# Two attention blocks on one core: the last two images rearranged over DMA queues and PSUM banks

## What is computed

```python
def stage_a(x, w_qkv, w_proj, b_proj):
    q, k, v = split(x @ w_qkv)                       # 8 heads of 32, windows of 32 tokens
    attn = softmax(q @ k.T * 32 ** -0.5)
    return (attn @ v) @ w_proj + b_proj

def stage_b(x, Wq, Wk, Wv, gamma):
    energy = einsum('bid,bjd->bij', x @ Wk, x @ Wq)  # 1024 x 1024 for each image
    return gamma * (softmax(energy) @ (x @ Wv))

x = x + stage_a(_gn(x), ...)
x = x + stage_b(_gn(x), ...)
```

## Time and profile before

| what | us |
|---|---|
| median of 3 runs | 668.62 |
| the 3 runs | 664.68, 668.62, 669.41 |
| profiled execution, its own time | 666.09 |
| its span, first to last instruction | 664.3 |
| PE busy | 592.8 (89%) |
| DVE busy | 467.3 (70%) |
| ACT busy | 348.4 (52%) |
| POOL busy | 198.7 (30%) |

### The profile page before, as it was taken

How to read it: one execution, slowest core, us unless ns; L and a number is a source line. 1 busy time by engine, 2 the same in 40 slices (tenths; PEclk the granted TensorE clock), 3 DMA queues, 4 the chain that set the end, 5 groups by cost and what they waited for, 6 DMA issues and landing times.

```text
span 664.3 us, 15166 instructions
## 1 busy us (share of the span) xinstructions
PE 592.8 (89%) x5859; PEld 428.8 (65%) x5859; DVE 467.3 (70%) x765; ACT 348.4 (52%) x486; POOL 198.7 (30%) x198
## 2 busy tenths in 40 slices
PE   2888855899999999999999999999999999876887
PEld 2465732457785777568776778577766767654656
DVE  4565477587867787788868787878868875754562
ACT  2664243485268644874278535865387414631462
POOL 7423322302351315320450335231442142002203
PEclk9999977799999999999999999999999999887989
DMA  6122422133224313223223313331322232201001
GB/s 204 32 58 69 125 64 62 44 78 97 71 67 111 95 27 97 81 60 108 59 75 87 95 44 91 99 87 44 97 72 57 53 81 65 52 1 58 33 0 64
DMA packets 40116, 47.53 MB, mean 72 GB/s; under 512 B 6848, under 2 KB 32064, under 8 KB 40064
## 3 DMA queue, kind: packets, MB, share of 16 engines
q1 hardware_dynamic: 35312, 41.57, 23.8%
q10 hardware_dynamic: 4624, 4.98, 2.3%
q0 software_dynamic: 128, 0.26, 0.1%
HBM read 10.09 MB, written 8.39 MB: 28 GB/s over the span
## 4 chain that ended last, share of the span: by engine, by line
PE 70%; DVE 14%; ACT 5%; issue 4%; DMA 3%; SPq 2%; ACTq 0%; POOL 0%; POOLq 0%; DVEq 0%
PE pb L296 10%; PE pb L298 9%; PE pb L297 9%; PE pa L296 6%; PE pa L297 6%; PE pa L298 6%; PE pa L576 5%; PE pb L630 4%; PE pb L648 4%; DVE max_neg L1110 3%; PE pa L543 3%; PE pb L462 2%; PE pa L462 2%; DVE bst L1005 2%; ACT e L896 1%
## 5 line engine op out<-in xcount | busy, mean ns | idle before, releaser
L296 PE MATMUL pb<-v_h,e_h 128*128 128x257 f16 x448 | 123.9, 277 | 0.0
L298 PE MATMUL pb<-v_h,e_l 128*128 128x257 f16 x448 | 122.8, 274 | 0.0
L297 PE MATMUL pb<-v_l,e_h 128*128 128x257 f16 x448 | 122.5, 273 | 0.0
L1110 DVE TENSOR_REDUCE max_neg<-pb 128x1 f32<-128x1024 f32 x64 | 77.8, 1218 | 57.8 <-PE pb L630 57.6
L1125 DVE TENSOR_TENSOR e_l<-e,e_h 128x1024 f16<-128x1024 f32 x64 | 77.9, 1224 | 19.8 <-ACT e L896 18.4
L905 ACT ACTIVATE qk_h<-pb,y_fac 128x256 f32<-128x256 f32 x56 | 26.5, 472 | 108.8 <-DVE y_fac L1132 108.4
L896 ACT ACTIVATE e<-pb,f_energy 128x1024 f32<-128x1024 f32 x64 | 71.3, 1113 | 17.0 <-PE pb L648 17.0
L1331 POOL TENSOR_TENSOR y<-qk_h,y 128x256 f32<-128x256 f32 x64 | 45.9, 724 | 104.6 <-ACT qk_h L905 104.5
L1312 POOL TENSOR_TENSOR xb<-xin,bias 128x2048 f32<-128x2048 f32 x8 | 36.3, 4532 | 120.2 <-DVE x L1090 119.5
L1317 POOL TENSOR_TENSOR before_turn<-before_turn,a_rinv 128x1024 f32<-128x1024 f32 x16 | 30.6, 1915 | 113.3 <-DVE a_rinv L1071 107.9
L630 PE MATMUL pb<-q_stack,k_stack 96*128 96x512 f16 x128 | 40.6, 400 | 17.7 <-DVE max_neg L1110 8.2
(11 more groups left out here) (153 smaller groups left out, 1373.8 us busy)
## 6 DMA issues: line engine op xcount, KB each, us to landing
diag<-qkT SPq DMA_DIRECT2D x64, 128.0 KB, 2.4
xin<-in_x SPq DMA_DIRECT2D x15, 512.0 KB, 4.8
diag<-turned SPq DMA_DIRECT2D x60, 128.0 KB, 2.4
turned<-before_turn SPq DMA_DIRECT2D x118, 64.0 KB, 2.0
out<-y SPq DMA_DIRECT2D x24, 256.0 KB, 2.2
out<-y ACTq DMA_DIRECT2D x8, 256.0 KB, 2.1
q_stack<-qk_hl SPq DMA_DIRECT2D x8, 128.0 KB, 2.3
k_stack<-qk_hl SPq DMA_DIRECT2D x7, 128.0 KB, 2.4
```

Source lines behind the costliest of these rows:

```text
L296: nc.tensor.matmul(out_ap, lh, rh, start=start, stop=False)
L297: nc.tensor.matmul(out_ap, lh, rl, start=False, stop=False)
L298: return nc.tensor.matmul(out_ap, ll, rh, start=False, stop=stop)
L1110: nc.vector.tensor_reduce(max_neg[:, it:it + 1], energy_banks(b, it).rearrange("p a n -> p (a n)"), X, ALU.max, negate=True).then_inc(b_ma ...
```

## The change

- Regrouping of image 7: rows 0 and 1 (eight DMAs) stay on SP's queue, rows 2 and 3 (eight) go to POOL's, ahead of `b_keep(6, 3)`, with a semaphore of their own (`a_oxp`). The stacks of image 7: two DMAs on SP's queue, two on POOL's (`b_stackp`).
- Projection of image 7 in pa 0 to 3, without the wait for the residual two steps back.
- Step 6 has its own order on PE, ACT and DVE: no pairs of image 6 before the projection and transposes of image 7 are done; then pairs for tiles 0 to 3; the queries and keys of image 7 in pb 2 and 3; and pairs of jt 0 to 6 for tiles 4 and 5, ahead of the first energy. ACT copies all four transposes ahead of exponential 5.
- Image 6's tiles 6 and 7 are in pa 2 and 3. Energies of image 7: tiles 2, 4 and 6 in pa 0 and 1, the others in pb 0 and 1, each waiting for the maximum two before it. Values 0 to 2 of image 7 are made in `first(7)`.
- Turned energies of image 7 alternate between pb 0, 1 and pb 2, 3 and wait for the exponential two before. Behind each exponential only tiles 0 to 3 are made; tiles 4 to 7 come at the end, eight pairs each, in pb 0 to 3.
- The last tile of image 7 is scaled and added by one DVE instruction (`b_finish`) instead of one on ACT and one on POOL.

The core of the diff (semaphore declarations and the arguments that carry a bank's name are left out):

```diff
         def proj_bank(b, j):
-            return pb[:, (2 + j) % 4, :] if image(b, 0) else pa[:, 2 + j % 2, :]
+            if image(b, 0):
+                return pb[:, (2 + j) % 4, :]
+            return pa[:, j, :] if last_image(b) else pa[:, 2 + j % 2, :]
         def energy_banks(b, it):
...
                 return pb[:, 2:4, :]
+            if last_image(b) and it > 1 and it % 2 == 0:
+                return pa[:, 0:2, :]
             return pb[:, 0:2, :]
...
+        def value_bank(b, j):
+            return pb[:, 2 + j % 2, :]
+        def qk_bank(b, c):
+            return pb[:, 2 + c, :] if last_image(b) else pb[:, c, :]
+        def energy_T_banks(b, jt):
+            return pb[:, 2:4, :] if last_image(b) and jt % 2 == 1 else pb[:, 0:2, :]
         def split3(out_ap, lhs, rhs, start=True, stop=True):
...
         def result_bank(b, it):
             if last_image(b):
-                return pa[:, it, :] if it < 4 else pb[:, (it - 2) % 4, :]
-            if next_to_last(b) and it < 4:
-                return pa[:, it, :]
+                return pa[:, it, :] if it < 4 else pb[:, it - 4, :]
+            if next_to_last(b) and not 4 <= it < 6:
+                return pa[:, it if it < 4 else it - 4, :]
             return pb[:, 2 + it % 2, :]
...
             def second(i, b, o, m, f):
                 more = f and not (isinstance(i, int) and i + 3 >= IMAGES)
-                if m: a_regroup(sp, i + 1, range(4))
+                if m: a_regroup(sp, a_ox, i + 1, (0, 1) if last_image(i + 1) else range(4))
                 if more and not m: load(i + 3)
...
                 if more and m: load(i + 3)
-                if m: b_stacks(sp, i + 1)
+                if m: b_stacks(sp, b_stack, i + 1, (0, 2) if last_image(i + 1) else range(4))
             sp.dma_start(xin[:, 0:TPC, :], x_v[0, 0:TPC].rearrange("t p c -> p t c")).then_inc(a_load[0], 16)
...
             def a_projection(b, b_next, js):
                 for j in js:
-                    regrouped(pe, b, (j % 2,))
+                    if last_image(b) and j % 2 == 0:
+                        pe.wait_ge(a_ox, nth(b - 1, 256, 128))
+                    elif last_image(b):
+                        pe.wait_ge(a_oxp, 128)
+                    else:
+                        regrouped(pe, b, (j % 2,))
                     if image(b, 0) and j >= 2:
                         pe.wait_ge(a_ve, nth(1, 4, j + 1))
-                    elif j >= 2:
+                    elif j >= 2 and not last_image(b):
                         pe.wait_ge(a_x1, nth(b, 4, j - 1))
...
                     pe.wait_ge(a_ve, nth(b, 4, 7 + c))
+                elif last_image(b):
+                    pe.wait_ge(n_["b"]["ve"], nth(b, 1, 1))
                 else:
                     after(pe, b_exp, nth(b, 8, 0))
-                project_T(pb[:, c, :], wqk1_h, wqk1_l, slice(0, P), c, b_nh, b_nl).then_inc(b_qk, 1)
+                project_T(qk_bank(b, c), wqk1_h, wqk1_l, slice(0, P), c, b_nh, b_nl).then_inc(b_qk, 1)
             def b_project_v(b, js):
                 for j in js:
-                    if j < 2:
+                    if last_image(b) and j < 2:
+                        pe.wait_ge(b_part, nth(b - 1, 8, 5 + j))
+                    elif j < 2:
                         after(pe, b_part, nth(b, 8, j - 1))
...
+                        last = project(value_bank(b, j)[:, t * CH:(t + 1) * CH], (b_nh[:, :, tok], b_nl[:, :, tok]), wv1_h, wv1_l, slice(0, CH))
                     last.then_inc(b_v, 1)
             def b_energy(b, it, b_next):
-                pe.wait_ge(b_stack, nth(b, 64, 64))
...
                     pe.wait_ge(b_max, it - 1)
+                elif last_image(b) and it == 2:
+                    pe.wait_ge(b_part, nth(b - 1, 8, 2))
+                elif last_image(b) and it > 2:
+                    pe.wait_ge(b_max, nth(b, 8, it - 1))
                 else:
...
                     pe.wait_ge(b_rows, nth(b, 1, 1))
+                elif last_image(b) and jt == 1:
+                    pe.wait_ge(b_vl, nth(b, 4, 4))
+                elif last_image(b):
+                    pe.wait_ge(b_exp, nth(b, 8, jt - 1))
                 else:
...
                 for c in range(CHUNKS):
-                    last = nc.tensor.matmul(pb[:, c, :], q_stack[0:98, jt * P:(jt + 1) * P],
+                    last = nc.tensor.matmul(energy_T_banks(b, jt)[:, c, :], q_stack[0:98, jt * P:(jt + 1) * P],
                                             k_stack[0:98, c * CHUNK:(c + 1) * CHUNK], start=True, stop=True)
...
                     pe.wait_ge(b_el, nth(b, 8, jts[-1] + 1))
+                    if it >= 4:
+                        pe.wait_ge(b_exp, nth(b, 8, 8))
+                elif next_to_last(b):
+                    pe.wait_ge(b_el, nth(b, 8, jts[-1] + 1))
                     if it >= 6:
-                        pe.wait_ge(b_exp, nth(b, 8, 8))
-                elif next_to_last(b) and it < 4:
-                    pe.wait_ge(b_el, nth(b, 8, jts[-1] + 1))
-                elif next_to_last(b):
-                    if it >= 6:
-                        pe.wait_ge(b_part, nth(b, 8, it - 1))
+                        pe.wait_ge(b_part, nth(b, 8, it - 3))
+                    elif it >= 4:
+                        pe.wait_ge(b_qkl, nth(b + 1, 2, 2))
                 elif jts[0] == 0:
...
                     last.then_inc(b_pv, 1)
+            def last_first(i):
+                b_energy(i, 0, False)
+                outputs_behind(i - 1, (7,))
+                b_energy(i, 1, False)
+                b_energy(i, 2, False)
+                b_output(i - 1, 6, True, range(0, 4))
+                b_energy(i, 3, False)
+                b_output(i - 1, 6, True, range(4, 8))
+                b_energy(i, 4, False)
+                b_output(i - 1, 7, True, range(0, 4))
+                b_output(i - 1, 7, True, range(4, 8))
+                b_energy(i, 5, False)
+                b_project_v(i, (0, 1))
+                b_energy(i, 6, False)
+                b_project_v(i, (2,))
+                b_energy(i, 7, False)
             def first(i, b, o, m, f):
+                if last_image(i): return last_first(i)
                 for it in range(4):
-                    if o and b and not next_to_last(i - 1): b_output(i - 1, it, b, range(0, 4))
-                    if next_to_last(i - 1): b_output(i - 1, 4 + it // 2, b, range(it % 2 * 4, it % 2 * 4 + 4))
+                    if o and b: b_output(i - 1, it, b, range(0, 4))
                     if b and it == 2: b_energy(i, 1, m)
-                    if o and b and not next_to_last(i - 1): b_output(i - 1, it, b, range(4, 8))
+                    if o and b: b_output(i - 1, it, b, range(4, 8))
                     if f and it == 1: transposes("a", i + 2, range(4))
...
                     if o and last_image(i - 1):
-                        if it >= 6: b_output(i - 1, it, b)
+                        b_output(i - 1, it, b)
                         continue
-                    if next_to_last(i - 1): b_output(i - 1, 4 + it // 2, b, range(it % 2 * 4, it % 2 * 4 + 4))
-                    elif o: b_output(i - 1, it, b, range(0, 4))
+                    if o: b_output(i - 1, it, b, range(0, 4))
                     if f and it == 5: group_mean("a", i + 2)
...
                     if b and it == 7: b_energy(i, it, m)
-                    if o and not next_to_last(i - 1): b_output(i - 1, it, b, range(4, 8))
+                    if o: b_output(i - 1, it, b, range(4, 8))
                     if b and it < 7: b_energy(i, it, m)
             def outputs_behind(b, jts, its=range(6)):
                 for jt in jts:
-                    if jt == 0:
-                        pe.wait_ge(b_vl, nth(b, 4, 4))
-                        pe.wait_ge(a_ol, nth(IMAGES, 2, 0))
+                    pe.wait_ge(b_vl, nth(b, 4, jt // 2 + 1))
                     for it in its:
                         b_output(b, it, False, (jt,))
+            def next_to_last_second(i):
+                b_project_v(i, (0,))
+                b_max_rows(i)
+                b_project_v(i, (1,))
+                b_energy_T(i, 0)
+                b_project_v(i, (2,))
+                b_energy_T(i, 1)
+                b_project_v(i, (3,))
+                b_energy_T(i, 2)
+                b_energy_T(i, 3)
+                a_projection(i + 1, False, (0, 1))
+                b_energy_T(i, 4)
+                a_projection(i + 1, False, (2,))
+                transposes("b", i + 1, (0, 1))
+                a_projection(i + 1, False, (3,))
+                b_energy_T(i, 5)
+                transposes("b", i + 1, (2, 3))
+                outputs_behind(i, (0, 1, 2), range(4))
+                group_mean("b", i + 1)
+                outputs_behind(i, (3,), (0, 1))
+                group_var("b", i + 1)
+                outputs_behind(i, (3,), (2, 3))
+                b_energy_T(i, 6)
+                outputs_behind(i, (4,), range(4))
+                for c in range(CHUNKS):
+                    b_project_qk(i + 1, False, c)
```

(81 more changed lines are left out.)

76 lines of the change are left out of this document (39 added, 37 removed).

## The result

| | before | after |
|---|---|---|
| median, 22 runs each | 664.5 us (663.04 to 669.41) | 661.92 us (659.48 to 664.58) |
| ratio after to before | | 0.9947, 95% interval 0.9933 to 0.9962 |
| span of the profiled execution | 664.3 us | 660.4 us |

The ratio is 3.5 us on 664.5; the two medians alone differ by 2.6 us. The kernel is faster by half a per cent, less than the 1% that was named as the bound between "faster" and "the same", and it is clear of zero only because 22 runs stand on each side.

What follows compares the result with a forecast made beforehand. PE bounds the kernel, busy 89% of the span, with 28.0 us idle or at half clock after 557.6 us. A span gain of 5.6 less 1.3 for half clock gives 668.62 - 4.3 = 664.3 us, range 659.3 to 669.0.

Steps and rivals of the forecast that it cites:

- Regrouping: Image 7's regrouping DMAs, on two queues, land at 567.3 and 567.7 us; PE wants them at 569.0.
- third rival: POOL's regrouping DMAs held up by DVE, 2.5 us an issue, projection 1 9.7 us late: 674.0 us; chance 0.03.
- Projection: Projection of image 7: half clock kept up to 572.7 us, last transposes end at 579.1, before 583.2.
- Normalisation: Image 7's statistics chain: `normalise` starts at 586.2 instead of 593.0, 6.8 us earlier; 2.1 us given away ahead of `group_mean`.
- PE as the bound: First energy of image 7 at 601.5 instead of 605.6, stacks there before; with fewer pairs left, 7.4 us ahead.
- Energies: Image 7's energies up to the row maxima: `b_max_rows` at 619.1 against 624.0; 7.5 us ahead so far.
- Turned energies of image 7: Last image's exponentials: circle of 5.4 us over two jt, 3.55 of it PE work; of 7.5 us ahead 4.8 left.
- Half clock: PE's clock falls once in the last image, costing 1.3 us of the 5.6 us span gain.
- The end: Last matmul to store: one DVE instruction, issue at 656.0 to 656.1; span ends at 658.7, 5.6 us less.
- (1): No cost by the clock, as the fall comes where PE waits anyway: 5.6 us gain, 663.0 us; chance 0.2.
- (2): Clock falls again and again in the last image and once at 589: 1.2 us gain, 667.4 us; chance 0.15.
- (4): More gain than summed: hand-placed waits of 1 us are shorter, up to 3 us: 661.3 us; chance 0.19.

Runs made afterwards that it cites:

- group mean early: Changed kernel with image 7's group mean behind eight pairs of image 6 instead of twelve, and the group variance behind twelve: median 662.54 us, ratio 0.9973.
- filled gaps: Changed kernel with matmuls that feed nothing put into two of PE's gaps in the last image (14 and 20): median 660.52 us, ratio 0.9954.

## Why the prediction was right, point by point

The forecast was 4.3 us less, ratio 0.9936; measured is 0.9947, 3.5 us less. As a difference: the base of the forecast, 668.62 us, was the median of three runs, and over 22 it is 664.5, so the forecast of 664.3 us for the changed kernel is right as a gain and not as a time. That the span came out at 660.4 where 660.0 was forecast is in part luck: 0.9 us of it were there before the change begins. The sum of both distances is free of this: 100.8 before, 97.8 and 97.7 in the two profiles of the changed kernel, 3.0 us less where the walk has 4.3. By its steps:

- *Regrouping* was right: issued from 559.94 and 560.54 on, and PE did not wait for it. POOL took 4.31 us for eight, 0.54 each against 0.58 in the sum; the third rival (POOL held up by DVE) did not happen. One argument against it was misread: the prediction says that POOL issued four at 68 us "while DVE worked", and in the trace DVE has nothing in that stretch. It is this trace that bears on it:

```profile
68.19:70.52 2.33, 1.49 (x24) 1.15 (x25) 0.00 (x0) 0.00 (x0) 2.33 (x4) 1.00 0.84 225
560.54:564.85 4.31, 3.37 (x28) 2.42 (x28) 1.92 (x2) 3.61 (x5) 4.31 (x10) 1.00 0.78 229
```

  (The kernel before, then the changed one; columns as in the earlier trace rows.) DVE is busy for 1.92 of the 4.31 us. What the walk did not have is that the two queues slow each other.
- *Projection.* I kept the half clock of before at turned energy 3. In the first profile it did not come, in the second it did; 57.4 and 59.0 are on either side of the 58.2 of the walk (619.1 less 560.9), so that the middle fits is owed to two opposite misses.
- *Normalisation* was right: 584.31, which is 24.3 us behind turned energy 0 of image 6; the walk had 586.2, 25.3 behind, with the half clock that this profile doesn't have. `b_qk_low` 7.4 us behind `normalise`, as before. The 2.1 us given away ahead of `group_mean` were real and worth 1.0 at the row maxima (group mean early).
- *PE as the bound* was right: the first energy waits for nothing. That the stacks gained by POOL was wrong in size and did no harm, since they are covered.
- *Energies* were right: row maxima 1.73 us late for PE (1.9 in the walk), energy banks worth 1.2.
- *Turned energies of image 7* were right in kind and a little short: from the pairs of jt 2 to those of jt 4 it is 5.2 us, and on to those of jt 6 5.5, circle and idle time as worked out (from jt 0 to jt 2 it is 7.0, with half clock). At full clock the walk gives 37.0 for distance 2 and the kernel with filled gaps 37.6.
- *Half clock* is the term that was mis-sized. I took one fall at 1.3 us. One does cost 1.3, but there are two in half of the profiles: 1.3 to 2.6 us. The walk with its one fall has 38.3 for distance 2, measured are 40.3 with two and 38.8 with one; 0.6 us of each is the line above. Together with distance 1 that is the 1.3 us by which the gain in the profiles falls short of the forecast; the 0.8 us by which the ratio does lie within its interval.
- *The end* was right: 0.87 against 0.85 in the sum.
- *The account of before* was loose in one place. Of the 28.0 us lost it gives 13.7 to four waits and "the rest" to half clock. By the busy column of the earlier trace rows PE is idle for 16.6 of the 102.3 us, and 11.4 is what it is busy beyond the priced work. Nothing in the sum rests on it. The range's upper end has 1.6 us of spread where the lower has 2.0.

Of the rivals, (1) no cost by the clock is against the distances (37.6 with the gaps filled, 38.7 to 39.1 with one fall, 39.8 and more with two). (2) had the right direction, two falls instead of one, and not the size: 1.2 us of gain against 3.5. The Trainium skill's page "TensorE: Matmul & The Clock Gate", section "A second HAM failure mode: psum-queue depth-cycling", speaks of a clock that goes back and forth under brief waits between groups of matmuls; here it fell once or twice at the beginning of the last image, after waits of 1.7 and 2.4 us, and then stayed up through the circles with waits of 1.4 to 1.6 us each, so the trace agrees in part. (4), more gain than summed, did not come; the waits of "about 1 us" that it doubted are 1.09, 1.59, 0.66 and 0.94 us. What the prediction did not see, though its numbers held it, is that the circle of 5.4 us was a matter of two lines: it counted turned energy jt+2 as "queued behind the pairs of jt" and went on.

## What to carry to other kernels

When a second pair of banks lets a producer run ahead, the next production must also stand ahead of the consumer's work in the in-order queue; here the second pair was laid out and then blocked by the order, and exchanging two lines was worth 4.3 to 5.2 us by the ratios, more than the whole change (3.5). Multiply out every circle (who waits for whom, in queue order) and compare it with the busiest engine's work in it: 5.4 us against 3.55 was a warning that something other than the work set the pace. Before you credit a second pair of banks, compare with the old order at the same clock: here the mended order only came back to what the old one had. A second DMA queue gained nothing here where the transfers were covered, and where they were not (the stacks in the kernel before) the time from first issue to first use went from 4.3 to 4.7 us instead of down.

## What the runs showed of the hardware

- The clock's fall after the same wait of 2.38 us comes in some executions of a kernel and not in others. Where it comes, turned energy 3 and the two projections behind it take 4.61 us instead of 3.06. It moves a single profile of this kernel by 1.6 us, as much as several of the parts that were tested.
- DMAs issued on SP and POOL at the same time landed later than on SP alone: SP's second stack DMA, 64 KB, took 3.0 us against 2.0 in the changed order, and 3.9 against 2.8 in the kernel before (where two stores follow on SP's queue either way); in the changed kernel SP's eight regrouping DMAs took 3.1 us to landing (median) where sixteen on one queue took 2.0. POOL starts its first one 0.55 to 0.6 us behind SP on the same semaphore.
- POOL's issues took 0.54 us each with DVE busy for 1.92 of the 4.31 us, and 0.58 each with DVE idle: no slowing is seen. A DVE that is busy throughout, or one in the casts of e_h, did not coincide with them, so that is not shown.
